# Moving the back-transpose of the normalised attention output from the end of the odd step to the place between scores and transposed scores of the next even step

## What is computed

```python
# layer 0 (layer 1 is the same, with affine layernorm weights and one MLP in place of the experts)
h = modulate(ln(x), shift, scale)
q, k, v = split_heads(h @ w_qkv + b_qkv)          # 16 heads of 9
attn = softmax(q @ k.T * 9 ** -0.5)               # 128 x 128 for each batch and head
o = (attn @ v).merge_heads() @ w_proj + b_proj
x = x + gate_msa * o
xn = modulate(ln(x), shift2, scale2)
x = x + gate_mlp * moe(xn)                        # 4 experts, top 2; layer 1: gelu(xn @ fc1) @ fc2
```

## Time and profile before

| | |
|---|---|
| median of 3 runs | 471.15 us (469.41 to 471.58) |
| the profiled execution, its own time | 473.57 us |
| span of its instructions | 471.8 us |
| mean granted TensorE clock | 0.964 |
| TensorE busy (matmuls) | 418.1 us, 89% |
| VectorE, ScalarE, GpSimd busy | 279.7, 270.8, 127.9 us |
| attention of layer 0 | about 60 to 156 us in the span |
| attention of layer 1 | about 331 to 430 us in the span |

### The profile page before, as it was taken

The page is one execution under the profiler, slowest core; times in us unless marked ns, Lnnn a source line. Parts: engine busy times, 40 slices in busy tenths (PEclk is TensorE's granted clock), DMA queues, the critical chain, the costliest instruction groups (busy, mean ns, idle before and its releaser), DMA issues.

```text
span 471.8 us, 10743 instructions
## 1 busy us (share of the span) xinstructions
PE 418.1 (89%) x4010; PEld 337.3 (71%) x4010; DVE 279.7 (59%) x798; ACT 270.8 (57%) x515; POOL 127.9 (27%) x213
## 2 busy tenths in 40 slices
PE   3956599698889999999999999999799997999997
PEld 1514478566676779878976897799668675768885
DVE  7856577477966327349632664157776556774652
ACT  4524367887576690273058335903778764877562
POOL 3003134243211063026007400723152432121000
PEclk9978579989999999999999999999899999999999
DMA  7945455546543300000010114203346565210212
GB/s 213 195 117 171 119 167 132 140 105 173 156 114 97 82 1 1 27 0 1 0 27 0 33 46 147 104 2 77 94 117 178 152 158 160 76 42 1 51 51 75
DMA packets 51570, 42.51 MB, mean 90 GB/s; under 512 B 33595, under 2 KB 43762, under 8 KB 51514
## 3 DMA queue, kind: packets, MB, share of 16 engines
q1 hardware_dynamic: 51450, 41.80, 32.7%
q10 hardware_dynamic: 68, 0.02, 0.0%
HBM read 33.20 MB, written 8.29 MB: 88 GB/s over the span
## 4 chain that ended last, share of the span: by engine, by line
PE 58%; DMA 10%; DVE 8%; ACT 7%; SPq 7%; issue 6%; POOL 3%; DVEq 0%; ACTq 0%; POOLq 0%
PE bank L1680 14%; PE bank L1698 4%; PE bank L1560 3%; PE s_pair L1518 3%; DMA KA<-qk_scratch 3%; SPq L685 3%; PE st_pair L1541 3%; DMA QA<-mT 3%; PE bank L1451 2%; PE s_pair L1458 2%; PE s_pair L1459 2%; PE s_pair L1462 2%; PE s_pair L1465 2%; PE st_pair L1458 2%; DMA hid<-mT 2%
## 5 line engine op out<-in xcount | busy, mean ns | idle before, releaser
L1251 DVE TENSOR_REDUCE mx<-s_pair 128x8 f32<-128x1024 f32 x62 | 75.7, 1221 | 43.5 <-PE s_pair L1518 43.1
L954 ACT ACTIVATE pr<-st_pair 128x1024 f32<-128x1024 f32 x64 | 65.6, 1025 | 30.8 <-PE st_pair L1541 30.4
L1680 PE MATMUL bank<-w_sb,hid 128*128 128x144 f32 x640 | 80.6, 286 | 1.0 <-DVE aT L1330 1.0
L1680 PEld LDWEIGHTS bank<-w_sb,hid 128*128 128x128 f32 x640 | 79.6, 190 | 1.8 <-DVE aT L1330 1.2
L1003 ACT ACTIVATE hid<-s_pair 128x512 f32<-128x512 f32 x40 | 23.3, 612 | 51.4 <-PE s_pair L1465 51.4
L1560 PE MATMUL bank<-pr,V 128*10 128x128 f32 x1024 | 41.7, 282 | 0.0
L1518 PE MATMUL s_pair<-KA,QA 81*128 81x128 bf16 x400 | 33.3, 230 | 7.5 <-DMA KA<-qk_scratch 4.9
L1541 PE MATMUL st_pair<-QA,KA 83*128 83x128 bf16 x416 | 34.0, 228 | 6.6 <-DMA QA<-mT 6.6
L783 POOL TENSOR_TENSOR rstd<-var_eps,minus_half 128x4 f32<-128x4 f32 x16 | 16.2, 1014 | 84.7 <-DVE var_eps L1205 84.6
L1518 PEld LDWEIGHTS s_pair<-KA,QA 81*128 81x128 bf16 x400 | 26.0, 103 | 13.1 <-issue 8.9
L822 POOL TENSOR_TENSOR xs<-xs,tmp 128x144 f32<-128x144 f32 x32 | 17.1, 533 | 67.3 <-DVE tmp L1272 42.1
(11 more groups left out here) (280 smaller groups left out, 951.1 us busy)
## 6 DMA issues: line engine op xcount, KB each, us to landing
QA<-qk_scratch SPq DMA_DIRECT2D x25, 324.0 KB
KA<-qk_scratch SPq DMA_DIRECT2D x75, 108.0 KB
qk_scratch<-parts SPq DMA_DIRECT2D x16, 288.0 KB, 3.7
g_att<-gate_scratch SPq DMA_DIRECT2D x16, 144.0 KB, 4.9
g_mlp<-gate_scratch SPq DMA_DIRECT2D x8, 288.0 KB, 3.6
hid<-qk_scratch SPq DMA_DIRECT2D x6, 324.0 KB
hid<-qk_scratch SPq DMA_DIRECT2D x18, 108.0 KB
qk_scratch<-parts SPq DMA_DIRECT2D x16, 96.0 KB, 3.4
```

The costliest lines, as they stand in the source:

```text
L954: sc.activation(pr[:, Pn % 2, :], st_pair[:, :], ACT.Exp, scale=SCALE).then_inc(s["exp_s"], 1)
L1251: v.tensor_reduce(mx[:, HP * h:HP * (h + 1)], src[:, :].rearrange("p (h k) -> p h k", k=SEQ), AX.X, ALU.max).then_inc(s["max_s"], 1)
L1680: last = te.matmul(dst, hid[:, at:at + SEQ], w2_sb[:, MT1 * e + i, :], start=(i == 0), stop=(i == MT1 - 1))
```

## The change

ATT_T is no longer yielded at the end of the odd step. In the next even step it stands after MAX and before SCORE. The last one that this leaves over (batch 14 of a layer) is yielded at the head of `attention_end`. Nothing is added or removed; the semaphores and their values stay the same.

```diff
             if p + LEAD < NP:
                 yield "MAX", P0 + p + LEAD
+            if h == 0 and 0 <= b - 2:
+                yield "ATT_T", B0 + b - 2
             if p > 0:
                 yield "SCORE", P0 + p
             yield from mid
@@
             if 0 <= p - 1:
                 yield "PV", P0 + p - 1
             yield from post
-            if h == 1 and 0 <= b - 1:
-                yield "ATT_T", B0 + b - 1
 
         def attention_end(L):
 
             B1 = BATCH * (L + 1)
+            yield "ATT_T", B1 - 2
             yield "PV", NP * (L + 1) - 1
             yield "PROJ", B1 - 2
```

## The result

The changed kernel takes 474.92 us (median of 15 runs), the kernel before in the same comparison 472.19 us (median of 15). The ratio is 1.007, 95% interval 1.0046 to 1.0095: slower by 3.3 us, 2.2 to 4.5. The forecast was +3.9 us, to 475.1 us. The medians are of all runs, while the ratios leave out as slow those over 1.5% above the fastest of their kernel, which here cuts through one continuous spread; by the medians of what is left the three distances are 3.3, 1.7 and 3.5 us. The profiled execution spans 475.2 us, its mean granted clock is 0.95 (0.964 in the profile of before).

What follows compares the result with a forecast made beforehand. TensorE, 89% busy, was no bound by itself; the last chain also ran through transfers, SyncE, VectorE and ScalarE. Charges along it, 1.88 us in layer 0 and 2.06 in layer 1, gave 471.15 + 3.9 = 475.1 us, range 471.7 to 478.0.

Steps and rivals of the forecast that it cites:

- The wait for `an`: ATT_T's wait at the even step's head, 5.5 us of idle matmuls: removal gains nothing, MAX_T's later-released wait replaces it, +0.1 us per hole.
- The sign in VectorE's queue: VectorE's `row_max` of even halves was to start about 0.2 to 0.27 us earlier behind the odd step's PV.
- rival of the wait won: Holes at ATT_T close because `an` and the split are both there by MAX's end: -4.4 us, 466.8 us, chance 0.07.
- The copy of `aT`, +0.18 in each undisturbed step: Only SCORE stands between ATT_T and PROJ, so PROJ waits for ScalarE's copy: +0.18 us for each moved transpose.
- ScalarE late, 0.25 in batches 11, 12, 16, 27, 28: Where ScalarE is already late, copying `mT` first puts 0.27 us more before `aT`; charged +0.25 us per step.
- SCORE held by `mT`, 0.2: Batches 7, 23 and 25: `m_out` waits for the load and now precedes `a_out`, delaying PROJ by 0.2 us each.
- Batches 10 and 26, 0.28: Steps with a hole at TensorE's head: 0.18 us for PROJ's wait for `aT` plus 0.1 for the hole's growth.
- Batch 9, 0.45, held at MAX: A load holds MAX, so ATT_T's 0.27 us follow it exposed, plus 0.18 for `aT`: +0.45 us; also batches 4 and 20.
- cover by transfers: Eleven batches (0 to 3, 5, 6, 8, 19, 21, 22, 24) lie under transfers and issues: charged 0, at most 2.5 us.
- rival of the hidden case: Every TensorE delay is taken up by the next transfer or earlier `row_max`: +0 to +2.3, middle 472.3 us, chance 0.23.
- rival of the earlier maxima: MAX_T and `m_out` go earlier, shortening SyncE's six layer 1 waits for `mT`: 3.2 us back, +0.7, 471.9 us, chance 0.06.
- Full exposure (+6.4): Rival: no delay is covered, and stores of parts and their loads move back too: +6.4, 477.6 us, chance 0.13.

## Why the prediction was right

**Direction and mechanism.** *The wait for `an`* was priced at nothing won. Its row went and a row for the split came with 6.9 us in place of 5.5. The hole's growth of about 0.1 us was shown alone where ATT_T stood between MAX_T and MAX: 0.10 in batch 10 against that kernel's steps without a hole. The sign in VectorE's queue came too: in batches 2, 3, 18 and 19 the even half's `row_max` starts 1.33 to 1.35 us behind PV's start, before 1.58 or 1.59. The rival of the wait won fell, and with it the -4.4 us that follow from the listed wait alone: more time for `an` gave nothing, because the next semaphore in line came 0.11 us later.

**The copy of `aT`, +0.18 in each undisturbed step.** It was read from batch 13 of the kernel before. Measured 0.18 to 0.20 in batches 2, 10, 18 and 22, and taken away whole (2, 18, 22) by putting MAX back between the two. This term is shown. But batches 2, 18 and 22 are among those that the prediction charged nothing. Their steps are longer all the same, and whether a later transfer gives that back is not shown.

**Size.** The forecast of +3.9 lies inside the interval of the first comparison (2.2 to 4.5), but over three comparisons the medians differ by 2.3 to 2.9 us, and at equal granted clock it is +1.9 (1.3 to 2.5). The sum was a third to a half too large, and that the first ratio came out so near to it was in part luck. These terms of it were mis-sized:

- *ScalarE late, 0.25 in batches 11, 12, 16, 27, 28.* Measured 0.13 to 0.15 in the four that repeat. I took 0.27 us as the distance from one copy to the next, from the row in which `aT` goes first (131.18 to 131.45). With `mT` first it is 0.16, since that copy is the shorter one. The changed kernel in batch 12:

```profile
142.59 0.25 ACT L941 COPY mT<-bank 32x128 bf16<-32x128 bf16 x1
142.75 0.36 ACT L968 COPY aT<-bank 128x256 f32<-128x256 f32 x1
...
143.16 0.30 PEld L1594 LDWEIGHTS bank<-wo_r,aT 128*128 128x128 f32 x2 [0.34 <-ACT aT L968]
```

- *SCORE held by `mT`, 0.2.* By the same distance of 0.16 it is 0.07: in all three traces of the changed kernel, batch 7 and batch 23 have 0.51 or 0.52 us from SCORE to PROJ, where undisturbed steps of the kernel before have 0.44 or 0.45. Batch 25 was charged the same, but no trace of the changed kernel holds its SCORE; it has 0.63, as an undisturbed step, so 0.18.
- *Batch 17, 0.18.* Measured 0.04 or 0.05. Its SCORE to PROJ has the full 0.62 or 0.63; I take it that its predecessor's PROJ was already late, and a step counts only what is added to it.
- *Batches 10 and 26, 0.28.* Batch 10 measured 0.18 in two traces (in the third, 1.15, something else held it). Batch 26 has 0.31 or 0.32, but 0.14 of that appears between two traces of the kernel before, which leaves 0.18 too. The missing 0.10 is a cover that the prediction did not count ("with nothing to cover it"). In these two steps TensorE waits for VectorE at the head. Before, `tmp` of the batch ahead started 0.89 or 0.90 us behind PROJ's start in undisturbed steps, because VectorE was still at `row_max`: there was room for a later PROJ. Changed, `tmp` waits for PROJ and starts at 0.79 or 0.80. The odd half's `row_max`, on which both releases hang, follows at 2.15 or 2.16 us in place of 2.24 or 2.25. So VectorE took up 0.1 us of the late PROJ where a hole stands.
- *Batch 9, 0.45, held at MAX.* No trace of the changed kernel holds MAX there, and the step is 0.12 or 0.13 shorter in all three, while two traces of the kernel before differ by 0.05. Nothing of this term was seen.

Four batches less 0.11, two less 0.13, batch 25 less 0.02, batch 17 less 0.13 and batches 10 and 26 less 0.10 each make 3.94 - 1.05 = 2.9 us, and without batch 9 it is 2.4 us. The steps that repeat (2, 6, 10 to 12, 17, 18, 22 and 26 to 28) grew by 1.7 us together (batch 26 taken at 0.18), 0.9 of it in batches 10 to 12 and 26 to 28.

**What stays open.** The other two steps held at MAX (batches 4 and 20), at 0.45 each, and most of the cover by transfers were not measured: in those stretches two traces of one kernel differ by about as much as the terms or more. Which steps a load holds is itself not fixed: MAX of batch 4 is held in two of the three traces of the changed kernel, that of batch 20 in one. Whether the sum came out near the medians because these terms are right, or because errors in them cancel, the runs don't say. The rival of the hidden case reached to +2.3 us, so the time alone does not part it from the forecast. What speaks against it are the steps that grew. In part it may hold: at batch 9, and where batches 2, 18 and 22 may be covered later. The rival of the earlier maxima got no support: SyncE's wait for `mT` in layer 1 is 18.6, 13.9 and 14.9 us in the three traces against 16.7 and 16.9 before, and taking the head start away cost nothing. Full exposure (+6.4) is outside the interval of the first comparison.

## What to carry to other kernels

Before moving an instruction out of a wait, look at what takes its place at the head of the queue and when that is released: here both releases hang on one VectorE reduction and lie 0.11 us apart. Then look behind it: an instruction that another engine must answer before TensorE can go on (transpose, copy, product) lives on the work that stands between, so count that work before and after and hold it against the copy's time. A place elsewhere in the same kernel that already has the new order, as batch 13 here, prices it: it said 0.18 us, and 0.18 to 0.20 were measured.

## What the runs showed of the hardware

Two copies of ScalarE that are ready one behind the other start 0.27 us apart if the first takes 0.37 us, and 0.16 us apart if it takes 0.25: the second starts about 0.1 us before the recorded end of the first. One program's executions spread widely, and the spread goes with the granted clock: the kernel before took 465.75 to 476.52 us in 35 runs on one occasion, the shortest at a mean granted clock of 0.974, the longest at 0.950. In the fit above, 0.01 of mean granted clock goes with 3.4 us.
